# Row scores, 1/sqrt chains and attention values reordered in a fused attention and mixture-of-experts kernel

## The reference

```python
q = (layernorm(x) @ Wq + bq)        # 4 x 1024 x (16 heads x 16)
k = (ctx @ Wk + bk); v = (ctx @ Wv + bv)
attn = softmax(clip(einsum('bhqd,bhkd->bhqk', q, k) * scale, -1e4, 1e4))
x = x + einsum('bhqk,bhkd->bqhd', attn, v) @ Wo + bo
x = x + ffn(layernorm(x))           # shared SwiGLU expert + top 2 of 8 SwiGLU experts
```

## Time and profile before

| | us |
|---|---|
| median of 3 runs | 801.34 |
| lowest, highest | 788.44, 803.86 |
| the profiled execution, whole | 798.33 |
| its span, first to last instruction | 796.6 |
| mean granted clock of TensorE | 0.902 of 2.4 GHz |
| busy in the span: PE, DVE, ACT, POOL | 640.8, 449.6, 342.4, 384.2 |
| the first scores of attention start at | 139.73 |
| the first scores of unit 15 start at | 251.28 |

### The profile page before, as it was taken

One profiled execution on the slowest core, in us unless ns is written; L12 is line 12 of the kernel. 1 busy time (PEld: TensorE's weight loads), 2 busy tenths in 40 slices (PEclk: granted clock), 3 DMA queues, 4 the chain that ended last, 5 costly groups with the idle time before them and its releaser, 6 DMA issues.

```text
span 796.6 us, 15555 instructions
## 1 busy us (share of the span) xinstructions
PE 640.8 (80%) x5326; PEld 421.5 (53%) x5326; DVE 449.6 (56%) x908; ACT 342.4 (43%) x560; POOL 384.2 (48%) x318
## 2 busy tenths in 40 slices
PE   2667776888888437787478998999999999999991
PEld 1323322344455214444154556878777887887780
DVE  4846567466766425576997764545445444544440
ACT  3555462677767047644013453333334333333330
POOL 4484561588777301221001363564675666576544
PEclk9968696589999659998789999999999999999996
DMA  8300000021121524755100384474665666565642
GB/s 261 132 2 0 1 0 1 2 41 31 39 42 28 119 53 116 192 152 202 33 1 30 130 272 108 86 104 75 107 95 95 101 99 105 88 108 87 88 61 33
DMA packets 108171, 66.13 MB, mean 83 GB/s; under 512 B 82946, under 2 KB 101316, under 8 KB 108100
## 3 DMA queue, kind: packets, MB, share of 16 engines
q1 hardware_dynamic: 93268, 41.91, 21.7%
q0 software_dynamic: 14832, 23.24, 17.3%
HBM read 29.47 MB, written 17.96 MB: 60 GB/s over the span
## 4 chain that ended last, share of the span: by engine, by line
PE 58%; DVE 21%; ACT 6%; issue 5%; DMA 3%; SPq 2%; POOL 2%; another core or an unknown queue 0%; POOLq 0%; ACTq 0%; DVEq 0%
PE bank L1300 55%; DVE bank L955 3%; DVE arena L916 2%; DVE hidden L1235 2%; SPq L462 2%; DVE arena L867 1%; DVE arena L999 1%; PE bank L1609 1%; PE bank L1359 1%; DMA out<-w_stage,map_i 1%; DVE x_sb L992 1%; DMA x_sb<-in_x 1%; DVE arena L890 1%; ACT arena L793 1%; ACT arena L688 1%
## 5 line engine op out<-in xcount | busy, mean ns | idle before, releaser
L1300 PE MATMUL bank<-arena 128*128 128x34 f16 (+6 forms) x1284 | 130.5, 251 | 49.8 <-DVE bank L955 15.1
L1300 PE MATMUL bank<-qx,arena 128*128 128x256 f16 (+1 forms) x1584 | 155.3, 281 | 3.9 <-ACT arena L755 2.8
L629 POOL DMA_INDIRECT out<-w_stage,map_i x71 | 114.2, 1609 | 73.3 <-DMA out<-w_stage,map_i 37.8
L1300 PEld LDWEIGHTS bank<-qx,arena 128*128 (+1 forms) x1584 | 125.7, 99 | 25.3 <-ACT arena L755 5.1
L1300 PEld LDWEIGHTS bank<-arena 128*128 128x128 f16 (+2 forms) x1284 | 73.7, 107 | 108.1 <-issue 40.9
L1269 DVE TENSOR_TENSOR hidden<-bank,hidden 128x512 f32<-128x512 f32 x71 | 49.1, 691 | 107.1 <-ACT hidden L836 89.7
L642 POOL TENSOR_TENSOR arena<-w_stage,arena 128x1024 f16<-128x1024 f32 x12 | 26.5, 2205 | 171.4 <-ACT arena L748 171.3
L1300 PE MATMUL bank<-arena,w_stage 128*128 x852 | 104.6, 273 | 1.4 <-ACT w_stage L842 0.7
L1300 PE MATMUL bank<-arena,qx 128*128 (+1 forms) x316 | 85.2, 393 | 17.9 <-DVE arena L916 14.3
L836 ACT ACTIVATE hidden<-bank 128x512 f32<-128x512 f32 x71 | 42.4, 597 | 128.2 <-PE bank L1300 106.1
L616 POOL DMA_INDIRECT qx<-rows_d,map_i x71 | 71.9, 1013 | 51.5 <-DVE lane_w L1261 31.6
(11 more groups left out here) (187 smaller groups left out, 750.8 us busy)
## 6 DMA issues: line engine op xcount, KB each, us to landing
w_stage<-in_w_all SPq DMA_DIRECT2D x27, 512.0 KB, 4.2
x_sb<-in_x SPq DMA_DIRECT2D x8, 512.0 KB, 8.5
rows_d<-arena SPq DMA_DIRECT2D x8, 512.0 KB, 3.6
out<-x_sb POOLq DMA_DIRECT2D x8, 512.0 KB
qx<-rows_d,map_i POOLq DMA_INDIRECT x71
qx<-qx SPq DMA_TRANSPOSE x71
out<-w_stage,map_i POOLq DMA_INDIRECT x71
arena<-arena SPq DMA_TRANSPOSE x32, 2.5
```

Of the source, the lines that this page charges most:

```text
L629: pool.indirect_dma_start(out=out, out_offset=bass.IndirectOffsetOnAxis(ap=map_i[:, 1, i:i + 1], axis=0), in_=y_sb[:, r], in_offset=None, ...
L1300: return pe.matmul(o, a, b, start=first, stop=last, skip_group_check=not check)
```

## The change

- Stage before attention: three 1/sqrt chains instead of two (tiles 0 to 3, 4 to 11, 12 to 31; `CHAIN_OF` says which one a group waits for). ACT normalises group 0 first and then evacuates k, splits wq and copies bo (`project_inputs`). The fourth tile of a group is ACT's again. PE makes k without waiting for all constants. The high halves of the block keys move from DVE to POOL (`keys`), one batch at a time.
- Row scores of group n-1 go with iteration n for every n: three ahead of `query(n)`, four single ones between its q matmuls, one behind. The maxima of group n-2 are transposed in iteration n.
- Attention: `weigh` is called by rounds and is two units behind (`weigh(u-2, r)`), one round before each subtraction. `project` is four units behind and stands with two idle matmuls between the second and third subtraction; the other two idle matmuls are gone. DVE makes all four clips first, then the addition, moments, and `normalise(u-2)`; the addition is that of unit u-5. ACT makes four exponentials, then three casts, the high half of the attention values, and the fourth cast. p_f has 6 buffers, in the tile `hidden`; p_h and p_l have 3x4. The drain has 5 rounds.
- The splits of the first three weight blocks stand in the rounds 16 to 18; SP's three loads stand behind all its transposes of attention values.

The diff, cut to its core:

```diff
-            def unit(u):                       # PE
-                if known(u, 0):
-                    scores(u)
-                    keep_busy(2)
-                    subtract_max(u, 0)
-                    subtract_max(u, 1)
-                if known(u, 1):
-                    weigh(u - 1)
-                if known(u, 0):
-                    subtract_max(u, 2)
-                    subtract_max(u, 3)
-                    keep_busy(2)
-                if known(u, 3):
-                    project(u - 3)
+            def unit(u):
+                if known(u, 0):
+                    scores(u)
+                for r in range(RT):
+                    if r == 2:
+                        if known(u, 4):
+                            project(u - 4)
+                        if known(u, 0):
+                            keep_busy(2)
+                    if known(u, 2):
+                        weigh(u - 2, r)
+                    if known(u, 0):
+                        subtract_max(u, r)
...
-                clip(u, 0)                     # DVE
-                clip(u, 1)
-                if known(u, 4):
-                    residual(u - 4)
-                    moments(u - 4)
-                    mean_and_variance(u - 4)
-                clip(u, 2)
-                clip(u, 3)
-                if known(u, 1):
-                    normalise(u - 1)
-                if u in (4, 6, 8):
-                    split_lo(u // 2 - 2)
+                for r in range(RT):
+                    clip(u, r)
+                if known(u, 5):
+                    residual(u - 5)
+                    moments(u - 5)
+                    mean_and_variance(u - 5)
+                if known(u, 2):
+                    normalise(u - 2)
+                if NU <= u < NU + 3:
+                    split_lo(u - NU)
...
-                    exps(u, 0)                 # ACT
-                    exps(u, 1)
-                    cast_p(u, 0)
-                    cast_p(u, 1)
+                    for r in range(RT):
+                        exps(u, r)
+                    for r in range(RT - 1):
+                        cast_p(u, r)
...
                             ins = mm(bank[2 + hf][:, :], wq_hl[:, a, cc, bass.ts(hf, P)], xn_t[:, n % 2, c, cc],
                                      i == 0 and cc == 0, i == 2 and cc == HF - 1)
-                    ins.then_inc(q_ready, 1)
+                            if n > 0 and (i, cc) in ((1, 0), (2, HF - 1)):
+                                if (hf, i) == (HF - 1, 2):
+                                    ins.then_inc(q_ready, 1)
+                                row_scores(n - 1, (3 + 2 * hf + (i == 2),))
+                    if n == 0 or hf < HF - 1:
+                        ins.then_inc(q_ready, 1)
...
             for n in range(NG):
                 transpose_xn(n)
-                scores_with(n)
+                if n >= 2:
+                    max_t(n - 2)
+                if n >= 1:
+                    row_scores(n - 1, range(3))
                 query(n)
+                if n >= 1:
+                    row_scores(n - 1, range(7, HF * GT))
                 if 1 <= n <= B:
                     value_rows(n - 1)
-            scores_with(NG)
+            row_scores(NG - 1)
...
-            moments1(0)
-            scale_and_shift(slice(0, 2 * GT), moments1(1))
+            scale_and_shift(slice(0, GT), moments1(0))
+            moments1(1)
+            ins = moments1(2)
             dve.wait_ge(k_copied, HF)
...
+            scale_and_shift(slice(GT, 3 * GT), ins)
+            for g in range(3, NG):
                 ins = moments1(g)
-            scale_and_shift(slice(2 * GT, NT), ins)
+            scale_and_shift(slice(3 * GT, NT), ins)
```

More of the change, by code:

```diff
@@ L55, in build @@
     NBUF = 6
+    PB = 3
+    FB = 6
     OW = 2 * D + 2
@@ L178, in build @@
         used[0] = shared_from
-        p_f = carve([4, 512], F32)
-        p_h = carve([2, 4, 512], F16)
-        p_l = carve([2, 4, 512], F16)
+        p_h = carve([PB, 4, 512], F16)
+        p_l = carve([PB, 4, 512], F16)
         r_sum = carve([UT, HD], F32)
@@ L224, in build @@
         v_hh = hidden[:, B * C:B * C + B * C // 2].bitcast(F16).rearrange("p (b c) -> p b c", b=B)
+        p_f = hidden[:, :].rearrange("p (r n) -> p r n", r=FB)
         act_g = hidden[:, 0:2 * GC].rearrange("p (r n) -> p r n", r=2)
@@ L455, in _ @@
                                            ).then_inc(ot_got[v % 2], 16)
-                if v >= NU - 3:
-                    load_w(v + 7 - NU)
+            for q in range(4, 7):
+                load_w(q)
             def transpose_x2(g):
@@ L602, in unit @@
                         pool.wait_ge(ph_ready, k + 1)
-                        if u >= 2:
-                            pool.wait_ge(pv_ready, u - 1)
-                        pool.tensor_tensor(p_l[:, u % 2, r], p_f[:, r], p_h[:, u % 2, r],
+                        if u >= PB:
+                            pool.wait_ge(pv_ready, u - PB + 1)
+                        pool.tensor_tensor(p_l[:, u % PB, r], p_f[:, k % FB], p_h[:, u % PB, r],
                                            ALU.subtract).then_inc(pl_ready, 1)
@@ L667, in _, with project_inputs @@
         def _(act):
[L669 to L678, removed]
+            def project_inputs():
+                for hf in range(HF):
+                    act.wait_ge(k_ready, hf + 1)
+                    act.activation(k_f[:, hf], bank[hf][:, 0:BK], ACT.Identity, bias=bk_c[:, hf:hf + 1],
+                                   accum_out=q_sum[:, NG * HF + hf:NG * HF + hf + 1]).then_inc(k_copied, 1)
+                act.wait_ge(q_loaded, 16 * N_Q)
+                act.copy(wq_hl[:, 0], wq_f).then_inc(wq_hi, 1)
+                act.wait_ge(bo_ready, 1)
+                act.copy(bo_bc, bank[7][:, 0:C]).then_inc(bo_copied, 1)
+                act.wait_ge(const_ready, N_CONST)
             def normal(n):
-                act.wait_ge(moments_ready, 1 if n < 2 else 2)
+                act.wait_ge(moments_ready, CHAIN_OF[n])
                 if n >= 2:
@@ L730, in _ @@
             normal(0)
+            project_inputs()
             for n in range(NG):
@@ L739, in _ @@
                     copy_v(n - 2)
-            for j in range(NG - 4, NG):
+            for j in range(NG - 2, NG):
                 copy_max(j)
```

144 lines of the change are left out of this document (56 added, 88 removed).

## The result

The changed kernel takes **822.49 us** (median of 4 runs, 820.84 to 823.61) against 797.95 for the kernel before (4 runs, 788.44 to 803.86): a ratio of 1.039, 95% interval 1.0313 to 1.0467. The ratios of this document compare fast executions with fast ones (of the kernel before, here 788.44 and 794.56), so that they are not the quotients of the medians beside them, here 1.031. By the medians it is slower by 24.5 us, where the forecast said 12.9; 822.49 lies inside the range of 786 to 831, and inside that of the forecast's own case (803 to 825). The outcome that the forecast gave the largest chance, slower by less than 2% (0.48), did not come; slower by more had 0.43. The profiled execution took 821.68 us, its span is 819.9, the mean granted clock 0.86 (0.902 before).

What follows compares the result with a forecast made beforehand. Before attention no engine was full, PE going back and forth with DVE. Terms of -21 (before attention), +25.4 (ten units), +0.5 (first units) and +8 (tail) gave +12.9, so 814 us beside the median; range 786 to 831.

Steps and rivals of the forecast that it cites:

- rival B: Attention units: the clock stays down throughout, 11 us each, +34, kernel 827 us; chance 0.18.
- decides attention: Projection in each unit: waits for DVE's addition behind four clips, fourth exponential bare, unit 8.0 us instead of 7.22.
- A unit at 8.0 us at the higher clock: Attention unit at 2.4 GHz: 8.0 us instead of 7.22, with PE idle 1.45 us before the projection.
- The clock, +2.1 a unit: Attention units: lower clock through projection and idle matmuls in most units adds 2.1 us, giving 10.1.
- A: Rival for the attention units: the clock stays up, 8.0 us each, kernel 788 us, not slower; chance 0.15.
- C: Rival for the attention units: projection finds its addition done, 6.6 us a unit, kernel 772 us; chance 0.05.
- First units: First five attention units: 36.4 us against 35.9, +0.5, bounds -4 and +3.
- Tail: Drain from unit 15 to the last projection's end: one unit longer, 31.9 us against 23.8, +8.
- The start, "I take -2 there": Start up to the third iteration: first q earlier, most lost again behind the third chain; -2 us, bounds 0 and -7.
- The last stretch, 18.3 us: Last stretch before attention: loses the doubled block of row scores, 18.3 us against 27.6, -9.3.
- The iterations n = 2 to 6: Before attention: row scores between the q matmuls save 7.4 us for n = 2 to 4, 2.4 for n = 5 and 6.
- attention starting later than 127: Sign at the start of attention that the forecast is wrong; it expected a start near 119 us, 139.73 before.

Runs made afterwards that it cites:

- e4: Changed kernel with five more idle matmuls on PE ahead of the projection, inside its wait for the addition: 810.77 us, ratio 1.0153 to the kernel before.
- e3: Changed kernel with DVE's addition of unit u-5 between the second and third clip: 804.94 us, ratio 1.0067 to the kernel before.
- e9: Changed kernel with the edit of e3 and three idle matmuls ahead of each unit's scores from the sixth on: 787.44 us, ratio 0.9919 to the kernel before.
- e7: Changed kernel with the projection behind the attention values in the drain's five rounds: 823.9 us, ratio 1.03 to the kernel before.
- e8: Changed kernel with POOL's output bias additions for groups 0 and 1 behind its other work before attention: 827.84 us, run once.
- e5: Changed kernel with DVE's third 1/sqrt chain behind the row maxima of group 0: 817.46 us, ratio 1.0227 to the kernel before.
- e6: Changed kernel with DVE's split of wo and gate moved from group 5's row maxima into the first attention unit: 821.23 us, ratio 1.0271 to the kernel before.

## Why the prediction was right or wrong

- *Direction and range*: right, with the change 24.5 us instead of 12.9. The total would not have told the mechanism: 822.49 lies nearer to rival B's 827 than to 814, and only the units, 10.19 us against B's 11, speak for the forecast. The step that "decides attention" did decide it: project waits for y_added behind four clips, the fourth exponential is bare, and both are releasers in the trace.
- *A unit at 8.0 us at the higher clock*: right, 8.10 in e4. The wait of PE at the clock that was really granted is 1.12 us and not 1.45; at the higher clock, in e4, 1.43 us lie between the start of the idle matmuls in it and the projection (191.39 to 192.82).
- *The clock, +2.1 a unit*: right, 10.19 on average against 10.1. Projection 2.72 us (2.63 forecast), idle matmuls 0.86 from start to start (0.85), scores back at 0.83. Rivals A and B fall by the same rows; C was right about what the addition's place is worth, as e3 and e9 show, and wrong about where it stands.
- *First units*: +1.1 against +0.5. *Tail*: +8.3 against +8; the working has the projection in the way of unit 15's values, and e7 shows that with it gone the low halves hold them up.
- *The start, "I take -2 there"*: wrong, +6.9. The step has the right wait, the third row score behind the third chain, but no price for the chain ("No row prices that"); it takes 9.3 us beside POOL's work, where the last chain of the kernel before took 3.8. In e8, with 5.4 us for the chain, the third transposes still come 1.8 us later than the old ones: so the stretching is not the whole of the miss, and the chain's place has a part in it. Taken out of the way (e5), they come 3.1 us before the old ones; that this lies near -2 is in part luck, since no row stood behind that figure.
- *The last stretch, 18.3 us*: wrong, 25.7. "2.5 (DVE's value split, an estimate from its short operations)" was 3.5, and the split of wo and gate, which the sum put at nothing, was 6.2 us (105.59 to 111.76) ahead of the reductions; e6 takes 4.8 us of it away.
- *The iterations n = 2 to 6*: 13.4 us gained instead of 9.8. In e5, where they begin ten microseconds earlier, the same iterations gain 10.5 (40.2 to 98.5 us), near the forecast, so that about 3 of the 13.4 look like a return of the late start. This stretch is the good part of the change; that it is the row scores between the q matmuls was not tested by a run of its own.
- *Size of the whole*: the stage before attention missed by 12.5 us (-8.5 against -21), attention by 1.8, the feed-forward part by -3.8, and the profile's difference is 23.3 us. The sign "attention starting later than 127" was the one that went off, at 131.24. Of the signs of being right, a wait of 1.3 us or more was 1.12, and the last projection ended at 302.25 instead of near 288.
- *A slip*: by its own rule the chance of faster by over 2% is 0.10 (C's 0.05 and a third of A's 0.15), not 0.09.

## What to carry to other kernels

In this kernel a short chain of small operations on DVE cost its own time (0.18 us each) only while POOL was idle; beside POOL an operation could last as long as POOL's instruction (2.04 and 2.26 us), so look at what POOL does in that stretch before placing it ahead of something that PE waits for. In a loop whose engines are tied by semaphores, the place of one small operation (0.68 us here) can go with the clock of TensorE as well as with the length of the loop: price a wait at both clocks, and fill what remains of PE's waits with idle matmuls, at places where they cost nothing (0.78 us filled, 10.6 us gained over ten units).

## What was not expected of the hardware

- A DVE operation on 20 columns took 0.18 us with POOL idle and up to 2.26 us beside one of POOL's instructions, twelve times as long; the chain 3.8, 5.4 or 9.3 us according to what POOL did.
- The clock of a unit hung on less than a microsecond of PE's waits: with 0.78, 0.39 and 0.17 us of waits in 6.90 us some units of e3 fell and some did not (clock 0.75 over ten), with the 0.78 filled nine of ten held (0.98). In the kernel before, 12.2 us of waits in 40 pieces went with 0.95; in the changed one 23.2 us in 31 pieces with 0.65.
